# First layer of a graph kernel: two more edge tiles of 26 summed on TensorE, and the histogram's one-hot tables built on ScalarE

## The reference

```python
def scatter_mean(src, index, dim_size):
    s = segment_sum(src, index, num_segments=dim_size)
    cnt = segment_sum(ones((src.shape[0],)), index, num_segments=dim_size)
    return s / maximum(cnt, 1.0)[:, None]
edge_attr_agg = scatter_mean(edge_attr, edge_index[0], x.shape[0])
h = relu(concatenate([x, edge_attr_agg], axis=1) @ W1 + b1)
x = x + h @ W2 + b2
```

## Time and profile before

| what | value |
|---|---|
| three runs | 9415.41, 9416.3, 9416.7 us, median 9416.3 |
| profiled execution | 9417.29 us |
| its span, first to last instruction | 9415.4 us |
| mean granted TensorE clock over the span | 0.650 |
| busy over the span: PE, DVE, ACT, POOL | 54%, 63%, 24%, 61% |
| scatters of the first layer (L896) | 1240, mean 1546 ns |
| matmuls of `z_add` (L705) | 5580 |

### The profile page before, as it was taken

The page is one execution under the profiler, slowest core; times in us unless marked ns, Lnnn a source line. Parts: engine busy times, 40 slices in busy tenths (PEclk is TensorE's granted clock), DMA queues, the critical chain, the costliest instruction groups (busy, mean ns, idle before and its releaser), DMA issues. The chain is left out here.

```text
span 9415.4 us, 111015 instructions
## 1 busy us (share of the span) xinstructions
PE 5089.1 (54%) x30046; PEld 3768.9 (40%) x30046; DVE 5888.4 (63%) x17251; ACT 2271.3 (24%) x3961; POOL 5781.5 (61%) x5121
## 2 busy tenths in 40 slices
PE   5888888888478888456666666666444000000000
PEld 3554445445256666345555555555443000000000
DVE  6888888888499999366666666666544222222222
ACT  0111111111155555134444444444211000000000
POOL 4888888888400000367777777777430777777776
PEclk9888888888699999655555555555555555555555
DMA  3333333333300000023333333333310222222221
GB/s 80 34 37 34 35 36 34 37 34 29 68 3 4 4 4 3 18 55 56 57 57 56 56 57 57 56 57 57 69 43 21 48 55 51 52 52 53 54 52 47
DMA packets 616262, 402.42 MB, mean 43 GB/s; under 512 B 523613, under 2 KB 533114, under 8 KB 613150
## 3 DMA queue, kind: packets, MB, share of 16 engines
q0 software_dynamic: 303360, 197.19, 18.2%
q1 hardware_dynamic: 310430, 197.07, 7.2%
q10 hardware_dynamic: 2304, 6.55, 0.2%
HBM read 215.25 MB, written 185.18 MB: 43 GB/s over the span
## 5 line engine op out<-in xcount | busy, mean ns | idle before, releaser
L1736 POOL DMA_INDIRECT rows_l<-att_row_table,slots_l x2016 | 1998.2, 991 | 647.3 <-issue 613.8
L896 POOL DMA_INDIRECT acc<-val,idx x1240 | 1917.3, 1546 | 417.1 <-issue 373.6
L1007 POOL DMA_INDIRECT rows_l<-relation_table,idx x1612 | 1528.9, 948 | 777.5 <-issue 490.9
L1018 DVE SCALAR_TENSOR_TENSOR run<-run,mask,rows_l 128x64 f32<-128x64 f32 x1612 | 459.6, 285 | 1571.3 <-DMA rows_l<-relation_table,idx 1515.6
L705 PE MATMUL banks<-part 128*128 128x490 bf16 (+1 forms) x5580 | 1294.4, 391 | 0.0
L1054 PE MATMUL banks<-run,link 128*128 128x64 f32 x98 | 21.1, 421 | 2039.4 <-PEq L987 2039.4
L1850 PE MATMUL banks<-rows_l,prob 128*128 128x65 f32 x4032 | 918.7, 419 | 45.0 <-ACT piece_part L1786 41.5
L1850 PEld LDWEIGHTS banks<-rows_l,prob 128*128 128x128 f32 x4032 | 877.5, 330 | 105.8 <-issue 86.5
L1181 DVE TENSOR_SCALAR hot_code<-columns_bf,codes 128x196 bf16<-128x196 bf16 x3200 | 916.8, 287 | 0.0
L1180 DVE TENSOR_SCALAR hot_src_lo<-columns_bf,codes 128x128 bf16<-128x128 bf16 x3200 | 860.4, 269 | 25.4 <-PE banks L1288 24.2
L1054 PEld LDWEIGHTS banks<-run,link 128*128 128x128 f32 x98 | 21.0, 333 | 2040.1 <-issue 2040.1
(11 more groups left out here) (373 smaller groups left out, 9255.3 us busy)
## 6 DMA issues: line engine op xcount, KB each, us to landing
piece_sums<-kept_l SPq DMA_DIRECT2D x252, 264.0 KB, 4.4
running_sums<-run SPq DMA_DIRECT2D x62, 832.0 KB, 3.5
attr<-in_edge_attr SPq DMA_DIRECT2D x61, 624.0 KB, 3.7
rows_l<-att_row_table,slots_l POOLq DMA_INDIRECT x2016
rows_l<-relation_table,idx POOLq DMA_INDIRECT x1612, 2.5
acc<-val,idx POOLq DMA_INDIRECT x1240, 3.2
acc<-zero ACTq DMA_DIRECT2D x12, 512.0 KB, 16.0
quad_sums<-run SPq DMA_DIRECT2D x50, 64.0 KB
```

What stands on the lines that cost most here:

```text
L896: e.indirect_dma_start(acc_d[k], bass.IndirectOffsetOnAxis(ap=idx[h][:, r:r + 1], axis=0), val[h][:, r, :], None, compute_op=ALU.add).then ...
L1007: e.indirect_dma_start(gbuf[h][:, r, :], None, table, bass.IndirectOffsetOnAxis(ap=idx[h][:, r:r + 1], axis=0))\
L1018: e.scalar_tensor_tensor(run[h][:, r, :], before_row, mask[h][:, r:r + 1], row, ALU.mult, ALU.add).then_inc(s_step, 1)
L1736: e.indirect_dma_start(rows[u][:, r, :], None, hx_d, bass.IndirectOffsetOnAxis(ap=slots[u][:, r:r + 1], axis=0))\
```

## The change

HS goes from 20 to 18, so NZ from 6 to 8: a half scatters 18 tiles (groups of 4, 4, 4, 4 and 2) and sums 8 on PE. The two one-hot tables are no longer built by DVE but by ACT: the `dst` digits of the half are copied to a tile of their own, then for each column two activations write |iota - digit| (`Abs`, the digit as bias, scale -1), and after each part of five or six columns two activations turn this into relu(1 - |iota - digit|), which is one where they are equal and zero elsewhere. One part follows each of the five `val` copies. Where `high0` lies moves to another borrowed tile.

```diff
-HS = 20
+HS = 18
...
-            high0 = [borrow(0, NZ * W0, bf16).rearrange("p (r f) -> p r f", f=W0) for n in range(2)]
+            high0 = [borrow(1, NZ * W0, bf16).rearrange("p (r f) -> p r f", f=W0) for n in range(2)]
...
+            hdig = sb("dst_digits_of_half", [P, 2, HALF], f32, ctx)
+            one0 = sb("one_column", [P, 1], f32, ctx)
+            PARTS = [(c * HALF // NG, (c + 1) * HALF // NG) for c in range(NG)]
...
 @block.vector
+                    e.memset(one0[:, :], 1.0)
...
-                    e.sem_inc(s_hot, 1)
...
-                            e.wait_ge(s_hist, hh + 1)
-
-                            e.tensor_tensor(ohlo[h][:, :, :], bc(ps[7][:, 0:P].unsqueeze(1), [P, HALF, P]),
-                                            bc(dlo[:, bass.ds(t0, HALF)].unsqueeze(2), [P, HALF, P]), ALU.is_equal)
-                            e.tensor_tensor(ohhi[h][:, :, :], bc(ps[7][:, 0:HI].unsqueeze(1), [P, HALF, HI]),
-                                            bc(dhi[:, bass.ds(t0, HALF)].unsqueeze(2), [P, HALF, HI]),
-                                            ALU.is_equal).then_inc(s_hot, 1)
...
 @block.scalar
+                    e.sem_inc(s_hot, 1)
+
+                    def hot_part(hh, h, c):
+                        lo, hi = PARTS[c]
+                        if c == 0:
+                            e.wait_ge(s_hist, hh + 1)
+                            e.wait_ge(s_hd, hh + 1)
+                        for r in range(lo, hi):
+                            e.activation(ohlo[h][:, r, :], iota[:, :], ACT.Abs, bias=hdig[:, 0, r:r + 1], scale=-1.0)
+                            last = e.activation(ohhi[h][:, r, :], iota[:, 0:HI], ACT.Abs, bias=hdig[:, 1, r:r + 1], scale=-1.0)
+                        last.then_inc(s_apart, 1)
+                        e.wait_ge(s_apart, hh * NG + c + 1)
+                        e.activation(ohlo[h][:, lo:hi, :], ohlo[h][:, lo:hi, :], ACT.Relu, bias=one0[:, 0:1], scale=-1.0)
+                        last = e.activation(ohhi[h][:, lo:hi, :], ohhi[h][:, lo:hi, :], ACT.Relu, bias=one0[:, 0:1], scale=-1.0)
+                        if c == NG - 1:
+                            last.then_inc(s_hot, 1)
...
                             e.copy(high0[1], left0[0]).then_inc(s_high, 1)
+                            e.copy(hdig[:, :, :], digits[:, :].rearrange("p (c t) -> p c t", c=2)
+                                   [:, :, bass.ds(hh * HALF, HALF)]).then_inc(s_hd, 1)
...
                                 if k == 1:
                                     digits_of(hh, h)
+                                hot_part(hh, h, k)
```

More of the change, by code:

```diff
@@ L631, in build @@
                                          "dup", "targets", "val_free", "pace"))
-            s_high, s_left, s_spread, s_z, s_dig, s_digits = (
-                sem(f"l0_{n}") for n in ("high_parts", "rests", "spread", "z_added", "digits_staged", "digits"))
+            s_high, s_left, s_spread, s_z, s_dig, s_digits, s_apart, s_hd = (
+                sem(f"l0_{n}") for n in ("high_parts", "rests", "spread", "z_added", "digits_staged", "digits", "apart",
+                                         "dst_digits_staged"))
+            hdig = sb("dst_digits_of_half", [P, 2, HALF], f32, ctx)
+            one0 = sb("one_column", [P, 1], f32, ctx)
+            PARTS = [(c * HALF // NG, (c + 1) * HALF // NG) for c in range(NG)]
             s_add = [sem(f"l0_acc{k}") for k in range(NACC)]
```

## The result

The changed kernel takes 9676.6 us (median of four, 9674.7 to 9677.6) against 9416.5 before on the same chip: ratio 1.0275, 95% interval 1.0258 to 1.0293. It is slower by 260 us where 231 were forecast.

A forecast was written before the change was run, and what follows sets the result against it. POOL's scatters bound the kernel at 36.85 us a half; after the change the PE and DVE chain would, at 40.5. 62 x 40.5 + 5 = 2516 us against 2284.7, +231 on 9417.3, gives 9648; range 9480 to 9715.

The forecast's parts named there:

- The bound of before: First-layer loop: POOL's scatters set 36.85 us a half; the PE and DVE chain took 35.8, leaving 1 us at most.
- Piece C: From the start of z_add(3) to the next half's rest_one: 12.0 us after the change, 10.82 before.
- Piece A: From rest_one to the start of z_add(0): 12.9 us after the change, 9.50 before.
- Piece B: From the start of z_add(0) to that of z_add(3): 14.3 or 15.4 us after the change, 14.92 before.
- the upper walk: Sum of the three pieces of a half with a z_add(0) of 5.59 us: 40.3 us.
- The stretch without a `z_add`: On PE, from the first group's transposes to z_add(0): 9 us after the change, nearly as long as the 10 before.
- ACT: Tables on ACT: 17 us a half added to 3.97, between bounds of 7.6 and 25.2, costing nothing.
- The cover: PE's own pace between val copies, 4.7 us or more, hides ACT's work; gone above some 30 us a half.
- The upper bound on an `Abs`: ACT's table building, nothing overlapped: 0.366 and 0.301 us per Abs, taken from the Relu with bias.
- The rival of the full clock: PE keeps 2.4 GHz through the loop: 37.1 us a half, 9437 us in all, +20; chance 0.05.
- The faster rival: PE and DVE overlap better, POOL keeps setting the pace: 33.3 us a half, 9202 us, -215; chance 0.08.
- ACT as the bound: 15 table loads of 1.283 us add 19.2 us a half on ACT: about 9930 us, +510; chance 0.04.

The follow-up runs named there:

- twelve_scatters: Kernel before with 12 of the 20 scatters of a half issued, eight tiles left out of the sums; single run, 9332.3 us against 9389.2, mean half 35.85.
- rows_early: Changed kernel with the transposes of the next half's first group issued ahead of the last two z_add; ratio 0.9982 to the kernel before.
- tables_on_act: Changed kernel with HS set back to 20 (6 tiles on PE), tables still on ACT; ratio 0.9997 to the kernel before, mean half 36.79.
- more_abs: Changed kernel with 52 more Abs a half on ACT, into a tile nobody reads; ratio 1.0279 to the kernel before, mean half 40.95.
- after_filled: Changed kernel with 20 more matmuls of zeros a half on PE, where it waits for DVE; ratio 1.0034 to the kernel before.
- both_early: Changed kernel with next half's first transposes ahead of the last two z_add, and z_add(k - 1) right behind sums(k - 1); ratio 0.9763, 9165.3 us.
- the two moves: Kernel before with next half's first transposes ahead of the last two z_add and z_add(k - 1) right behind sums(k - 1); ratio 0.9991.
- eight_on_pe: Kernel before with 18 tiles scattered and 8 on PE, tables still on DVE; ratio 1.0267 to the kernel before, mean half 40.96.
- both_more_abs: `both_early` with 52 more Abs a half on ACT; ratio 1.0276 to the kernel before, mean half 40.95.
- z_early: Changed kernel with z_add(k - 1) issued right behind sums(k - 1), where it was z_add(k - 2); ratio 1.0048 to the kernel before.
- both_early_dve: `both_early` with the tables left on DVE, as in the kernel before; ratio 1.0128 to the kernel before, mean half 38.67.

## Why the prediction was right

*The bound of before* was as read. POOL held it at 36.85 and the chain stood 1 us behind: `twelve_scatters` gives 35.85 against the 35.8 that two halves had shown.

*Piece C*, 12.0 predicted, 12.13 measured. *Piece A*, 12.9 predicted, 13.17 measured, with the wait of 3.3 at the first comparison measured at 3.37; `rows_early` shows that it lay on the path in full. *Piece B*, 14.3 or 15.4 predicted, 15.58 measured.

*What was sized too small.* The prediction walked to 39.2 us with a `z_add(0)` of 4.46 and to 40.3 with one of 5.59, the two values of before, and took 40.5 a half for both and the hand-overs. In the changed kernel `z_add(0)` lasts 5.77 to 5.82 in 56 of 62 halves, so it is the upper walk that counts. The pieces add up to 40.88, 0.6 above that walk: 0.2 from `z_add(0)`, 0.3 in A and 0.1 in C. Taking nearly the upper value was a judgement that came out right, though the length it was based on was off. The stretch without a `z_add`, from the first transposes to `z_add(0)`, is 1040.47 - 1030.43 = 10.0 us after the change, not 9, and it was 135.05 - 123.89 = 11.2 before, not 10, by this line of the kernel before:

```profile
123.89 0.60 PE L685 MATMUL banks<-ident,src_tile 128*128 128x128 f32 x4
```

The longer stretch had the shorter `z_add(0)` behind it, 4.46 against 5.82, so its length alone does not tell how long `z_add(0)` will be. Why `z_add(0)` is slow in nearly every half, where in the kernel before it lasted 4.3 to 5.9, was not tested.

62 x 0.45 = 28 us is the difference between the forecast 9648 and the measured 9677. Two small terms beside it nearly cancel: 2.5 us ahead of the loop, for the digits of two more tiles a half, and some 2 us less in the loop, since its first halves take 40.2 to 40.9.

*ACT* is 23.8 us a half, 21 in the prediction (17 and the 3.97 of before), and costs nothing, as `tables_on_act` and `more_abs` show. The cover reaches further than the prediction's "some 30 us a half": in `more_abs` ACT is busy 34.7 us a half (1185.75 us in the 1400 from 1000 to 2400) and nothing is lost. What runs short first is not a `val` copy but the time until the next half's `rest_one`. The upper bound on an `Abs` was too low: 0.366 and 0.301 by the `Relu` with bias, 0.391 and 0.324 measured. It did not matter, because in a row they overlap. No row gave the 0.3 us that the upper bound put for a wait of ACT for its own results; in the changed kernel the `Relu` starts 0.04 us behind the last `Abs` of a part (1018.72 to 1018.76). `Abs` loads no table; the Trainium skill, "ScalarE: Activation LUTs", section on table sets, says that abs is in every set, and the trace now agrees for it as well.

*The rival of the full clock* (9437) describes what happens when PE is kept busy: `after_filled` is 0.34% over before, which the walk had at 0.2%. It fell as a forecast because PE was not kept busy. *The faster rival* (9202) named the right place, the first comparison behind `z_add(7)`, together with the low clock; with the order changed there the kernel runs at POOL's pace, 224 us faster than before. *ACT as the bound*, by table loads, has no support: the loop has none. With 11 us of activations more a half (52 x 0.22, start to start) ACT comes onto the path in `both_early`, and still not in the changed kernel.

## What to carry to other kernels

When a chain of two engines stands close behind the engine that sets the pace, moving work off the one and onto the chain needs the order in the chain looked at as well: ask what stands at the end of a round in one engine's program ahead of the instruction that the other engine needs first. A wait of TensorE can cost twice, once for the wait and once for what runs slowly behind it (3.7 us of 40.95 here); filling the wait with matmuls of zeros tells in one run how much the clock is worth. A part that shows no gain by itself (the tables on ACT, 0.9997; the two moves, 0.9991) may still be needed for the version that has one, because another engine's pace hid what it gave.

## What was not expected of the hardware

Kernels with different work settle on the same half: the changed kernel at 40.95 (40.92 and 41.00 in turn), `eight_on_pe` at 40.96, `more_abs` at 40.95 and `both_more_abs` at 40.95, though their waits differ in place and length. All of them have a slow stretch of PE's clock in each half; but so have `rows_early` (36.40), `z_early` (37.54) and `both_early_dve` (38.67), and they do not meet there. Why the four meet at one value was not tested. For a learner it is a warning: that two such kernels take the same time doesn't show that what differs between them is free. That ACT's work is free in `more_abs` is read from the waits above, not from the equal halves alone.

Short activations on ACT overlap: an `Abs` over 49 columns lasts 0.324 us, and a pair over 128 and 49 columns takes 0.52 from start to start, where the two durations add up to 0.715.
